# Small-head attentions: two PSUM banks for the scores and three for the turned scores, instead of three and two

## The chip, the cores and the metric

The kernel is one program on one core of a Trainium2 chip. The metric is the device time of one execution in microseconds (us). The core has a matrix engine (PE, TensorE), a vector engine (DVE, VectorE), a scalar engine (ACT, ScalarE), GpSimd (POOL) and DMA queues issued by SyncE (SP). Each engine runs its own instruction list in order and waits on semaphores that others raise. PE writes its results to PSUM, which has eight banks of 512 f32 columns in 128 partitions; DVE and ACT read them there.

## The reference

The program is a stack of four attentions and four feed-forwards on x of shape (4, 512, 128), each added to x. Three of the attentions have 16 heads of 8 channels and take a softmax over all 512 keys, and these are the ones that the change touches:

```python
x = x + _L0_attn_a_ref(_layernorm(x), ...)   # q and k normed per head, no mask
x = x + _L0_ffn_ref(_layernorm(x), ...)      # six layers of windowed attention and feed-forward
x = x + _L0_attn_b_ref(_layernorm(x), ...)   # q, k, v from a latent of 32, causal
x = x + _L0_ffn_ref(_layernorm(x), ...)
x = x + _L1_attn_a_ref(_layernorm(x), ...)   # linear attention
x = x + _L1_ffn_ref(_layernorm(x), ...)
x = x + _L1_attn_b_ref(_layernorm(x), ...)   # causal
x = x + _L1_ffn_ref(_layernorm(x), ...)

scores = einsum('bhsd,bhtd->bhst', q, k) / sqrt(8)
att = softmax(scores); out = einsum('bhst,bhtd->bhsd', att, v)
```

## The kernel before

`build` makes eight stages and `weave` interleaves their programs on each engine: a stage is a generator that yields once per step, and a guest stage starts when its host has taken a given number of steps. `small_attention(core, kind, ...)` is called three times, with kind "norm" (`_L0_attn_a_ref`, the first attention), "latent" (`_L0_attn_b_ref`, the second) and "plain" (`_L1_attn_b_ref`, the third). The other two kinds are causal. Between them runs `local_block` (the six-layer feed-forward), which takes most of the time; `linear_attention` and `swiglu` run ahead of and beside the third attention.

In `small_attention` one step k of the loop is one head of one batch (`ROW_ITEMS` = 4 batches x 16 heads = 64), and the work on a head is spread over steps. The scores are computed twice:

- `scores(k, n_)` (L1228 to L1246): queries on the partitions, keys along the row, in pieces of at most one bank. They serve only to find each query's maximum, which DVE takes from PSUM with `tensor_reduce` (L1463) into `nm`. Each piece raises `s_mm`, each maximum `max_done`.
- once per four heads the 16 maxima of each query are turned by PE (L1288, into `MISC_BANK`), cut into three bf16 parts on DVE (L1471 to L1481) and sent by DMA (L1048) into rows of `qs`.
- `turned_scores(k, n_)` (L1249 to L1265): the same product turned, keys on the partitions, with the negated maximum added by those rows. It runs `LAG` = 7 heads later. ACT takes the exponential from PSUM into `pt` (L1407). Each piece raises `st_mm`, each exponential `exp_done`.
- the value products (L1303) run once per four heads, over three steps: one block, one block, two blocks; then ACT keeps them (L1395) and DVE turns and normalises them (L1486 to L1496).

A head has `NP` pieces: four of 512 columns for "norm" (`q_pieces`, `k_pieces`, one per 128 queries or keys), three in the causal kinds (512; 128 and 384 together; 256), each with a mask product of 128 columns (L1243, L1262) ahead of each part. `Q_BANKS` are the banks through which the score pieces rotate, `K_BANKS` those of the turned pieces; a piece may start when the reader of the bank's last piece is done. With `AV_BANK`, `MISC_BANK` and `ROW_BANK` (the preparation of the next batch) all eight banks are in use.

On PE the order within a step is written out:

```python
for n_ in range(NP):
    if hs is not None:
        scores(hs, n_)
    if n_ == 1 and k % 4 == 0 ...:       # L1288, the maxima turned
    if ht is not None:
        turned_scores(ht, n_)
```

and behind it the value products, the output product (L1312, once per batch) and `prepare(k)` (the layer norm and q, k, v of the next batch, at 6 to 8 of a batch's 16 steps), then the guest stage's step. DVE's order in a step is: the maxima of the head, then in every fourth step the cut of the maxima and the turning of outputs, then its share of the preparation. ACT's order: keeping the products, the exponentials of the head seven earlier, its share of the preparation.

Of the kernel before, what the change touches and what calls it, by code (L numbers as in the profile page):

```python
# [10 lines left out]
ACT = mybir.ActivationFunctionType  # L11
AX = mybir.AxisListType
# [847 lines left out]
def normed_at(g, i):  # L860

    return 3 * g + g // SG + i
# [12 lines left out]
def small_attention(core, kind, local=None, linear=None, source=None):  # L875

    nc, d, x, z, ps = core.nc, core.d, core.x, core.z, core.ps
# [14 lines left out]
    width = 1280 if causal else 2048  # L892
    NP = len(q_pieces)
    if kind == "latent":
        Q_BANKS, K_BANKS, AV_BANK, MISC_BANK, ROW_BANK = (1, 2, 3), (4, 5), 6, 7, 0
    else:
        Q_BANKS, K_BANKS, AV_BANK, MISC_BANK, ROW_BANK = (0, 1, 2), (3, 4), 5, 6, 7
    LAG = 7
    RING = 8
    TURN_VW, MAKE_VW = -25, -24  # L900
# [9 lines left out]
    exp_done, out_kept = ev("sa_exp_done", "sa_out_kept")  # L910
    x_summed, centred, row_done, v_kept, max_done, mcut_done, out_normed, added = ev(
        "n_added", "n_centred", "n_done", "sa_v_kept", "sa_max_done", "sa_mcut_done", "sa_out_normed", "sa_added")
# [13 lines left out]
    def layer_at(k, at):  # L926

        l, s = divmod(k - at, 2)
        return l if kind == "norm" and s == 0 and 0 <= l < DEPTH else None
# [6 lines left out]
    def group_at(k, at):  # L936

        g, s = divmod(k - LAG - at, 4)
        return g if s == 0 and 0 <= g < ROW_GROUPS else None

    def head_at(k, lag):

        return k - lag if 0 <= k - lag < ROW_ITEMS else None
# [21 lines left out]
    nm = prep("nm", [P, 2, 4, TB])  # L965
# [6 lines left out]
    pt = heads_only("pt", [P, RING, width])  # L972
# [174 lines left out]
    def tensor(pe):  # L1147
# [79 lines left out]
        def scores(k, n_):  # L1227

            b, h = divmod(k, SH)
            i_ = NP * k + n_  # L1230
            if kind == "plain" and i_ == 0:
                linear.all_free(pe)
            if n_ == 0 and h == 0:
                pe.wait_ge(ld_low.sem, ld_low.at(16 * loads * (b + 1)))
            if n_ == 0 and h == SH // 2 and b == 0:
                pe.wait_ge(ld_high.sem, ld_high.at(16 * loads))
            if i_ >= 3:
                pe.wait_ge(max_done.sem, max_done.at(i_ - 2))
            bank = ps[:, Q_BANKS[i_ % 3], :]
            for i, col in q_pieces[n_]:  # L1240
                keys = P * (i + 1) if causal else SEQ
                if causal:
                    pe.matmul(bank[:, col + i * P:col + i * P + P], core.ident16[:, :], cmask[:, :], start=True, stop=False, skip_group_check=True)  # L1243
                last = pe.matmul(bank[:, col:col + keys], qs[b % 2][0:STACK, h, i * P:i * P + P], ks[b % 2][0:STACK, h, 0:keys],  # L1244
                                 start=not causal, stop=True, skip_group_check=True)
            last.then_inc(s_mm.sem, 1)  # L1246

        def turned_scores(k, n_):

            b, h = divmod(k, SH)  # L1250
            i_ = NP * k + n_
            if n_ == 0 and h % 4 == 0:
                g = k // 4
                pe.wait_ge(ld_m[g % 2].sem, ld_m[g % 2].at(16 * PARTS * (g // 2 + 1)))
            if i_ >= 2:
                pe.wait_ge(exp_done.sem, exp_done.at(i_ - 1))
            bank = ps[:, K_BANKS[i_ % 2], :]
            for j, col in k_pieces[n_]:
                q0 = P * j if causal else 0
                cols = part[j][1]  # L1260
                if causal:
                    pe.matmul(bank[:, col:col + P], cmask[:, :], core.ident16[:, :], start=True, stop=False, skip_group_check=True)  # L1262
                last = pe.matmul(bank[:, col:col + cols], ks[b % 2][0:M_ROW + PARTS, h, j * P:j * P + P],  # L1263
                                 qs[b % 2][0:M_ROW + PARTS, h, q0:SEQ], start=not causal, stop=True, skip_group_check=True)
            last.then_inc(st_mm.sem, 1)  # L1265

        for k in range(FIRST, LAST):
            if kind == "plain" and k == FIRST + 4:
                local.z_final(pe, BATCH - 1)
                pe.wait_ge(ld_w.sem, ld_w.at(16 * n_ld))  # L1270
                for s in range(3):
                    last = pe.transpose(ROW[:, s * P:s * P + P], tmp[:, s, :], core.ident[:, :])
# [5 lines left out]
# [3 lines that stand above are left out]
                if n_ == 1 and k % 4 == 0 and 0 <= k // 4 - 1 < ROW_GROUPS:  # L1281
                    g = k // 4 - 1
# [8 lines left out]
            for at, blocks in AV_AT.items():  # L1291
                if (g := group_at(k, 4 + at)) is not None:
# [7 lines left out]
                    for j in blocks:  # L1300
                        off, cols = part[j]
                        for hh in range(4):
                            last = pe.matmul(ps[32 * hh:32 * hh + 32, AV_BANK, SEQ - cols:SEQ], va[:, g // SG % 2, j, 4 * (g % SG) + hh, :],  # L1303
                                             pt[:, (4 * g + hh) % RING, off:off + cols], start=j == 0, stop=j == TB - 1, skip_group_check=True)
# [9 lines left out]
            if (l := layer_at(k, TURN_VW)) is not None:  # L1314
# [4 lines left out]
                for c in range(8):  # L1319
                    last = pe.transpose(ps[:, c // 4, c % 4 * P:c % 4 * P + P], wv[l][:, c * P:c * P + P], core.ident[:, :])  # L1320
                last.then_inc(vw_mm.sem, 1)
            if (l := layer_at(k, MAKE_VW)) is not None:
# [5 lines left out]
                for c in range(8):  # L1328
                    for e in range(2):
                        u, j = divmod(2 * c + e, 4)  # L1330
                        rows = slice(64 * e, 64 * e + 64)
                        last = pe.matmul(ps[:, 2 + j, u * P:u * P + P], wvt[l % 2][rows, c, :], wo[l][rows, c, :], start=True, stop=True)
# [3 lines left out]
    def scalar(act):  # L1336
# [46 lines left out]
        for k in range(FIRST, LAST):  # L1383
            if k == FIRST:
                if kind == "latent":
                    local.early_free(act)
                if kind == "norm":
                    act.preload_act_table_set("natural_log_exp_and_others")
            if kind == "latent" and k == LAG:
                local.z_final(act, BATCH - 1)  # L1390
            if (g := group_at(k, 8)) is not None:
                act.wait_ge(av_mm.sem, av_mm.at(g + 1))
                if g >= 2:
                    act.wait_ge(out_normed.sem, out_normed.at(normed_at(g - 2, 1)))
                act.activation(ou[:, g % 2, :], ps[:, AV_BANK, :], ACT.Copy).then_inc(out_kept.sem, 1)  # L1395
            if (h := head_at(k, LAG)) is not None:
                if h == 0 and kind == "norm":
                    for i in range(2):
                        act.wait_ge(vw_stored[i].sem, vw_stored[i].at(16 * DEPTH // 2))
                if h >= RING:  # L1400
                    act.wait_ge(av_mm.sem, av_mm.at((h - RING) // 4 + 1))
                for n_, piece in enumerate(k_pieces):
                    i_ = NP * h + n_
                    col = part[piece[0][0]][0]
                    cols = sum(part[j][1] for j, _ in piece)
                    act.wait_ge(st_mm.sem, st_mm.at(i_ + 1))
                    act.activation(pt[:, h % RING, col:col + cols], ps[:, K_BANKS[i_ % 2], 0:cols], ACT.Exp).then_inc(exp_done.sem, 1)  # L1407
            prepare(k)
            if (l := layer_at(k, TURN_VW)) is not None:
                act.wait_ge(vw_mm.sem, vw_mm.at(2 * l + 1))  # L1410
                act.activation(wvt[l % 2][:, 0:4, :], ps[:, 0, :].rearrange("p (k c) -> p k c", c=P), ACT.Copy).then_inc(vw_kept_act.sem, 1)
            if (l := layer_at(k, MAKE_VW)) is not None:
                act.wait_ge(vw_mm.sem, vw_mm.at(2 * l + 2))
                if l >= 2:
                    act.wait_ge(vw_stored[l % 2].sem, vw_stored[l % 2].at(16 * (l // 2)))
                act.activation(wvo[l % 2][:, 0:2, :], ps[:, 2:4, :], ACT.Copy).then_inc(vw_kept_act.sem, 1)
                act.wait_ge(vw_kept_act.sem, vw_kept_act.at(2 * l + 2))
                act.wait_ge(vw_kept_dve.sem, vw_kept_dve.at(2 * l + 2))
                act.dma_start(core.wvo[l], pt[:, l % 2, :]).then_inc(vw_stored[l % 2].sem, 16)
            yield  # L1420

    def vector(dve):
# [10 lines left out]
        for k in range(FIRST, LAST):  # L1433
# [20 lines left out]
            if (h := head_at(k, 0)) is not None:  # L1454
                g = h // 4
                if h % 4 == 0 and g >= 2:
                    dve.wait_ge(mt_mm.sem, mt_mm.at(g - 1))
                for n_, piece in enumerate(q_pieces):
                    i_ = NP * h + n_
                    dve.wait_ge(s_mm.sem, s_mm.at(i_ + 1))  # L1460
                    for i, col in piece:
                        keys = P * (i + 1) if causal else SEQ
                        last = dve.tensor_reduce(nm[:, g % 2, h % 4, i:i + 1], ps[:, Q_BANKS[i_ % 3], col:col + keys], AX.X, ALU.max, negate=True)  # L1463
                    last.then_inc(max_done.sem, 1)
            if k % 4 == 0 and 0 <= k // 4 - 1 < ROW_GROUPS:
                g = k // 4 - 1
# [105 lines left out]
    def all_free(eng):  # L1572
        eng.wait_ge(added.sem, added.at(BATCH))

    stage = Stage(sync, gpsimd, tensor, scalar, vector)
    stage.early_free, stage.x_final, stage.row_free, stage.all_free, stage.row_bank = early_free, x_final, row_free, all_free, ROW_BANK
    return stage
# [500 lines left out]
```

## Time and profile before

| | |
|---|---|
| time, median of 3 runs | 4424.77 us (4423.37 to 4428.09) |
| time of the profiled execution | 4423.4 us |
| its span | 4421.6 us |
| mean granted TensorE clock | 0.962 |
| PE busy, in the span | 4099.9 us (93%) |
| DVE | 3431.0 us (78%) |
| ACT | 2902.9 us (66%) |
| POOL | 2305.1 us (52%) |
| L1463, maxima (768) | 378.5 us busy, 99.8 us idle before |
| L1407, exponentials (640) | 329.3 us busy, 189.4 us idle before |

The profile is one execution, seen by the hardware profiler. A timeline row gives the start in us from the span's start, the duration in us, the engine, the line of the kernel and the operation with what it writes and reads, how many instructions it merges, and in brackets how long the engine had been idle and what ended that. Several instructions of one line in a row are merged, and their duration is from the first's start to the last's end. A row of a stretch gives, after its bounds and length, the busy time of PE, PE's weight load, DVE, ACT and POOL with the number of instructions (those of one engine alone where only one was asked for), then the granted clock as a share of 2.4 GHz, the DMA share and GB/s. f32 matmuls are recorded as two instructions, and some matmul records are missing.

### The profile page before, as it was taken

Reading aid. Unit: us, or ns where it says so; the run is one execution under the profiler, and the core shown is the slowest. Engines: PE = TensorE matmul, PEld = TensorE weight load, DVE = VectorE, ACT = ScalarE, POOL = GpSimd, SP = SyncE. Lnnn points to the kernel's source line nnn. Section 1 sums busy time; section 2 is a strip of 40 time slices with the busy share of each in tenths; the row PEclk is TensorE's granted clock in tenths of the full one; section 3 lists DMA queues with packets and bytes.
Section 4 is the critical chain, followed back from the end, with each engine's and each line's share of the span. In section 5 each row is a group of like instructions: output and inputs, shape, how many; then the busy total and the mean of one; then the engine's idle time right before and its main releaser. Section 6 shows DMA issues by size and latency. Waiting matters only on the chain. (4 is left out here: it accounts for less than half of the span.)

```text
span 4421.6 us, 128540 instructions
## 1 busy us (share of the span) xinstructions
PE 4099.9 (93%) x53847; PEld 2028.2 (46%) x53847; DVE 3431.0 (78%) x5320; ACT 2902.9 (66%) x7265; POOL 2305.1 (52%) x1444
## 2 busy tenths in 40 slices
PE   5888999999999999998989999999999999988897
PEld 3222555555555554553434555555554555543442
DVE  3774888888888888885868888888888888865783
ACT  2654777777777777774546777777777777755453
POOL 3101766666666666664107666666666666631100
PEclk7987999999999999997989999999999999999898
DMA  5112000000000000001220000000000000001110
GB/s 167 48 30 63 2 2 26 3 21 7 21 7 2 21 7 2 2 2 45 67 66 7 2 21 7 21 7 2 26 2 21 7 2 2 2 10 32 44 45 10
DMA packets 68917, 97.79 MB, mean 22 GB/s; under 512 B 34472, under 2 KB 58756, under 8 KB 62340
## 3 DMA queue, kind: packets, MB, share of 16 engines
q1 hardware_dynamic: 67476, 83.28, 6.4%
q8 instruction: 426, 6.98, 0.7%
q10 hardware_dynamic: 864, 6.29, 0.4%
q14 instruction: 151, 1.24, 0.1%
HBM read 72.18 MB, written 16.78 MB: 20 GB/s over the span
## 5 line engine op out<-in xcount | busy, mean ns | idle before, releaser
L402 POOL TENSOR_TENSOR ra<-ra,rb 128x1024 f32<-128x1024 f32 x384 | 927.3, 2415 | 330.4 <-DVE rb L741 330.4
L416 POOL TENSOR_TENSOR qkr<-ra,inv 128x1024 f32<-128x1024 f32 x384 | 730.9, 1904 | 607.8 <-ACT inv L680 604.1
L448 PE MATMUL ps<-wvo,xs 128*32 128x512 f32 x6144 | 821.2, 606 | 72.2 <-ACT vs L602 72.2
L493 PE MATMUL ps<-wq,xs 128*128 128x512 f32 x1536 | 748.3, 610 | 6.2 <-DVE rb L741 3.5
L653 ACT ACTIVATE pr<-ps,neg 128x64 f32<-128x64 f32 x3072 | 668.1, 337 | 7.1 <-DVE neg L718 7.1
L602 ACT ACTIVATE vs<-ps 128x512 f32<-128x512 f32 x768 | 450.8, 587 | 227.2 <-PE ps L448 225.9
L515 PEld LDWEIGHTS ps<-kt,qt 64*32 64x32 f32 x24576 | 360.5, 107 | 293.8 <-issue 290.1
L718 DVE TENSOR_REDUCE neg<-ps 128x8 f32<-128x512 f32 x384 | 263.7, 687 | 279.8 <-PE ps L515 272.9
L493 PEld LDWEIGHTS ps<-wq,xs 128*128 128x128 f32 x1536 | 274.6, 191 | 431.6 <-issue 333.8
L738 DVE TENSOR_TENSOR ra<-ps,rope 128x1024 f32<-128x1024 f32 x384 | 451.7, 1176 | 24.3 <-ACT sq L627 17.3
L741 DVE TENSOR_TENSOR rb<-ps,rope 128x1024 f32<-128x1024 f32 x384 | 465.7, 1213 | 0.0
L764 DVE TENSOR_REDUCE ssq<-sq 128x16 f32<-128x1024 f32 x384 | 464.2, 1209 | 0.0
L541 PEld LDWEIGHTS ps<-vs,pt 128*32 128x32 f32 x11904 | 346.2, 110 | 239.9 <-issue 215.8
L1463 DVE TENSOR_REDUCE nm<-ps 128x1 f32<-128x512 f32 (+3 forms) x768 | 378.5, 549 | 99.8 <-PE ps L1244 97.7
L1407 ACT ACTIVATE pt<-ps 128x512 f32<-128x512 f32 (+1 forms) x640 | 329.3, 552 | 189.4 <-PE ps L1263 182.9
L435 POOL TENSOR_TENSOR pn<-pr,rden 128x512 f32<-128x512 f32 x384 | 400.4, 1043 | 47.3 <-DVE rden L724 41.7
L515 PE MATMUL ps<-kt,qt 64*32 64x64 f32 x24576 | 422.4, 218 | 0.3 <-DVE kt L772 0.3
L669 ACT ACTIVATE inv<-ssq 128x16 f32<-128x16 f32 x384 | 82.8, 216 | 507.5 <-DVE ssq L779 507.5
L541 PE MATMUL ps<-vs,pt 128*32 128x128 f32 x11904 | 407.2, 273 | 4.2 <-DVE pt L789 4.2
L627 ACT ACTIVATE sq<-ps 128x1024 f32<-128x1024 f32 x384 | 390.6, 1017 | 29.1 <-PE ps L493 28.0
L659 ACT ACTIVATE qt<-ps 128x512 f32<-128x512 f32 x384 | 244.5, 637 | 66.4 <-PE ps L560 62.5
L1244 PE MATMUL ps<-ks,qs 72*128 72x512 bf16 (+3 forms) x768 | 255.1, 354 | 26.0 <-DVE nm L1463 25.9
(253 smaller groups left out, 6246.0 us busy)
## 6 DMA issues: line engine op xcount, KB each, us to landing
wq<-in_L_ffn_Wqkv SPq DMA_DIRECT2D x12, 1024.0 KB, 5.2
wvo<-wvo_scratch SPq DMA_DIRECT2D x12, 1024.0 KB, 4.9
wvo_scratch<-pt ACTq DMA_DIRECT2D x6, 1024.0 KB, 4.0
w<-in_L_ffn_W SPq DMA_DIRECT2D x12, 341.0 KB
qs<-norm_pieces SPq DMA_DIRECT2D x9, 384.0 KB
ks<-norm_pieces SPq DMA_DIRECT2D x9, 384.0 KB
qs<-latent_pieces SPq DMA_DIRECT2D x9, 384.0 KB
ks<-latent_pieces SPq DMA_DIRECT2D x9, 384.0 KB
```

Source lines behind the costliest of these rows:

```text
L402: pool.tensor_tensor(ra[:, m % 2, :, :], ra[:, m % 2, :, :], rb[:, :, :], ALU.add).then_inc(sum_done.sem, 1)
L416: pool.tensor_tensor(qkr[:, m % 2, :, :].rearrange("p s (h c) -> p (s h) c", c=HD), ra[:, m % 2, :, :].rearrange("p s (h c) -> p (s h) c", ...
L435: pool.tensor_tensor(pn[:, m % 2, :, :], pr[:, m % 2, :, :], rden[:, m % 2, :, None].to_broadcast([P, 8, KEYS]), ALU.mult).then_inc(pn_don ...
L448: last = pe.matmul(VP[32 * j:32 * j + 32, :], xs[:, turn % 2, v * WIN:v * WIN + WIN], wvo[l % 2][:, j, :], start=True, stop=True)
L493: last = pe.matmul(PJ[:, qk, :], xs[:, turn % 2, t * P:t * P + P], wq[l % 2][:, at:at + 512], start=True, stop=True)
L515: last = pe.matmul(SB[32 * j:32 * j + 32, at:at + KEYS], qt[rows, m % 2, (2 * i + p) * TB + w, :], kt[rows, 4 * up + 2 * i + p, t * P + w ...
L541: last = pe.matmul(PO[32 * w:32 * w + 32, t * P:t * P + P], pt[:, m % 2, i * TB + w, half, :], vs[:, v, 2 * up + i, :], start=up == 0 and ...
L602: act.activation(vs[:, v, :, :].rearrange("p u c -> p (u c)"), VP, ACT.Copy).then_inc(v_kept.sem, 1)
L653: last = act.activation(pr[:, m % 2, n, :], SB[:, n * KEYS:n * KEYS + KEYS], ACT.Exp, bias=neg[:, m % 2, n:n + 1])
L738: dve.tensor_tensor(ra[:, m % 2, :, :].rearrange("p s (h c) -> p s h c", c=HD), both, table, ALU.mult)
L741: dve.tensor_tensor(rb[:, :, :].rearrange("p s (h e c) -> p s h e c", h=8, e=2), halves, tableh, ALU.mult).then_inc(rope_done.sem, 1)
L764: dve.tensor_reduce(ssq[:, m % 2, :], sq[:, :, :].rearrange("p s (h c) -> p (s h) c", c=HD), AX.X, ALU.add).then_inc(ss_done.sem, 1)
```

## The change

In both cases of the bank layout, one bank moves from `Q_BANKS` to `K_BANKS`. The indices and the two waits follow: a score piece waits for the maximum of the piece two earlier instead of three, a turned piece for the exponential of the piece three earlier instead of two. Nothing else differs.

```diff
     if kind == "latent":
-        Q_BANKS, K_BANKS, AV_BANK, MISC_BANK, ROW_BANK = (1, 2, 3), (4, 5), 6, 7, 0
+        Q_BANKS, K_BANKS, AV_BANK, MISC_BANK, ROW_BANK = (1, 2), (3, 4, 5), 6, 7, 0
     else:
-        Q_BANKS, K_BANKS, AV_BANK, MISC_BANK, ROW_BANK = (0, 1, 2), (3, 4), 5, 6, 7
+        Q_BANKS, K_BANKS, AV_BANK, MISC_BANK, ROW_BANK = (0, 1), (2, 3, 4), 5, 6, 7
...
-            if i_ >= 3:
-                pe.wait_ge(max_done.sem, max_done.at(i_ - 2))
-            bank = ps[:, Q_BANKS[i_ % 3], :]
+            if i_ >= 2:
+                pe.wait_ge(max_done.sem, max_done.at(i_ - 1))
+            bank = ps[:, Q_BANKS[i_ % 2], :]
...
-            if i_ >= 2:
-                pe.wait_ge(exp_done.sem, exp_done.at(i_ - 1))
-            bank = ps[:, K_BANKS[i_ % 2], :]
+            if i_ >= 3:
+                pe.wait_ge(exp_done.sem, exp_done.at(i_ - 2))
+            bank = ps[:, K_BANKS[i_ % 3], :]
```

In the same way L1407 reads `K_BANKS[i_ % 3]` and L1463 reads `Q_BANKS[i_ % 2]`.

## Rows read from the trace of the kernel before

**Rows 1.** Busy time by stretch: the three loops from first to last L1471.

```profile
102.80:362.70 259.90, 225.58 (x957) 60.12 (x956) 193.24 (x376) 146.96 (x260) 22.58 (x17) 0.86 0.16 44
2091.10:2264.70 173.60, 162.39 (x1419) 81.76 (x1418) 145.15 (x378) 99.54 (x199) 14.85 (x11) 0.96 0.22 63
4132.30:4334.10 201.80, 182.16 (x1460) 91.36 (x1458) 158.46 (x390) 110.73 (x213) 14.74 (x10) 0.95 0.17 46
```

**Rows 2.** Timeline of PE, first attention, one group at full clock.

```profile
300.24 0.39 PE L1244 MATMUL ps<-ks,qs 72*128 72x512 bf16 x1 [1.32 <-DVE nm L1463]
300.47 0.38 PE L1263 MATMUL ps<-qs,ks 75*128 75x512 bf16 x1
...
301.77 0.39 PE L1244 MATMUL ps<-ks,qs 72*128 72x512 bf16 x1
...
303.94 1.93 PE L1303 MATMUL ps<-pt,va 128*32 128x512 f32 x16
```

**Rows 3.** Timeline of DVE in the same group.

```profile
296.70 0.27 DVE L1471 COPY mf<-ps 16x128 f32<-16x128 f32 x1
...
299.50 2.48 DVE L1463 TENSOR_REDUCE nm<-ps 128x1 f32<-128x512 f32 x4
302.20 2.48 DVE L1463 TENSOR_REDUCE nm<-ps 128x1 f32<-128x512 f32 x4 [0.23 <-PE ps L1244]
306.23 4.88 DVE L1463 TENSOR_REDUCE nm<-ps 128x1 f32<-128x512 f32 x8 [1.54 <-PE ps L1244]
311.02 0.27 DVE L1471 COPY mf<-ps 16x128 f32<-16x128 f32 x1
```

**Rows 4.** Timeline of DVE, then of PE, second attention, one group.

```profile
2193.36 3.27 DVE L1463 TENSOR_REDUCE nm<-ps 128x1 f32<-128x512 f32 x8
2197.15 1.70 DVE L1463 TENSOR_REDUCE nm<-ps 128x1 f32<-128x512 f32 x4 [0.53 <-PE ps L1244]
...
2201.02 0.27 DVE L1471 COPY mf<-ps 16x128 f32<-16x128 f32 x1
...
2194.10 0.23 PE L1243 MATMUL ps<-cmask,ident 128*128 128x128 bf16 x1 [0.22 <-DVE nm L1463]
...
2195.88 0.86 PE L1303 MATMUL ps<-pt,va 128*32 128x256 f32 x16
2196.67 0.23 PE L1243 MATMUL ps<-cmask,ident 128*128 128x128 bf16 x1
```

**Rows 5.** Timeline of PE, first attention, two preparing heads.

```profile
179.48 0.39 PE L1263 MATMUL ps<-qs,ks 75*128 75x512 bf16 x1 [1.32 <-ACT pt L1407]
...
199.49 0.39 PE L1263 MATMUL ps<-qs,ks 75*128 75x512 bf16 x1 [0.58 <-ACT pt L1407]
```

**Rows 6.** Timeline of DVE, first attention, heads without turned scores.

```profile
93.14 9.79 DVE L1463 TENSOR_REDUCE nm<-ps 128x1 f32<-128x512 f32 x16
```

**Rows 7.** Timeline of PE in the three tails, one after the other.

```profile
363.64 0.61 PE L1263 MATMUL ps<-qs,ks 75*128 75x512 bf16 x1 [0.41 <-ACT pt L1407]
...
395.96 1.10 PE L1263 MATMUL ps<-qs,ks 75*128 75x512 bf16 x2 [0.32 <-ACT pt L1407]
...
2278.66 0.29 PE L1262 MATMUL ps<-ident,cmask 128*128 128x128 bf16 x1 [3.94 <-DMA qs<-mcut]
...
2292.86 0.23 PE L1262 MATMUL ps<-ident,cmask 128*128 128x128 bf16 x1 [0.41 <-ACT pt L1407]
...
4338.19 0.23 PE L1262 MATMUL ps<-ident,cmask 128*128 128x128 bf16 x1 [0.56 <-ACT pt L1407]
...
4343.98 0.29 PE L1262 MATMUL ps<-ident,cmask 128*128 128x128 bf16 x1 [3.95 <-ACT pt L1407]
...
4362.75 0.23 PE L1262 MATMUL ps<-ident,cmask 128*128 128x128 bf16 x1 [0.41 <-ACT pt L1407]
```

**Rows 8.** Busy time of two neighbouring groups, first attention.

```profile
299.50:313.80 14.30, 12.68 (x66) 3.24 (x66) 12.29 (x26) 9.43 (x18) 0.00 (x0) 1.00 0.01 3
313.80:331.00 17.20, 15.72 (x66) 3.75 (x66) 12.53 (x26) 9.60 (x18) 0.10 (x1) 0.80 0.00 1
```

More of the change, by code:

```diff
@@ L1406, in scalar @@
                     act.wait_ge(st_mm.sem, st_mm.at(i_ + 1))
-                    act.activation(pt[:, h % RING, col:col + cols], ps[:, K_BANKS[i_ % 2], 0:cols], ACT.Exp).then_inc(exp_done.sem, 1)
+                    act.activation(pt[:, h % RING, col:col + cols], ps[:, K_BANKS[i_ % 3], 0:cols], ACT.Exp).then_inc(exp_done.sem, 1)
             prepare(k)
@@ L1462, in vector @@
                         keys = P * (i + 1) if causal else SEQ
-                        last = dve.tensor_reduce(nm[:, g % 2, h % 4, i:i + 1], ps[:, Q_BANKS[i_ % 3], col:col + keys], AX.X, ALU.max, negate=True)
+                        last = dve.tensor_reduce(nm[:, g % 2, h % 4, i:i + 1], ps[:, Q_BANKS[i_ % 2], col:col + keys], AX.X, ALU.max, negate=True)
                     last.then_inc(max_done.sem, 1)
```

## The prediction

> **What bounds the kernel now.** The change touches only the loop over 64 heads in the three small-head attentions, so I began with the busy time per stretch, one stretch for each of the three [rows 1]. No engine is full: in the first, PE is busy for 225.6 of 259.9 us and DVE for 193.2; in the second 162.4 and 145.2 of 173.6; in the third 182.2 and 158.5 of 201.8. ACT is well below. Two engines near the top and neither full means that they wait for each other in turn, so shares say nothing and one repeating group has to be read instruction by instruction. A group is four heads. Names from here on: S0 to S3 are the score pieces of a head, T0 to T3 the turned pieces of the head seven earlier, R the maximum on DVE, E the exponential on ACT; the heads of a group are A, B, C, D, and D is the one after which DVE leaves the loop. PE's order is S0 T0 S1 T1 S2 T2 S3 T3, then the value products.
>
> The first attention's group at full clock [rows 2, 3]: DVE starts its side work (the cut of the maxima, the turning of outputs) at 296.70 and returns at 299.50, 2.80 later; the next side work starts at 311.02, so a group takes 14.32 us. While DVE is away PE fills the three score banks and stops: S3 of head A starts at 300.24 after 1.32 us idle, 0.74 after the start of the first R. So the bound is DVE's sum (its maxima and its side work) plus the gaps in which PE comes too late, 0.23 ahead of 302.20 and 1.54 ahead of 306.23. In both, PE was in the value products. What shortens those gaps is how far PE had run ahead in scores, and that is what the number of score banks sets.
>
> **The change part by part.** No instruction is added or taken away. Two waits move: S now waits for the R two pieces back (was three), T for the E three pieces back (was two). Behind a waiting S on PE stand T, the value products and everything woven in; behind a waiting T the same. The step is worked by replaying one group with the durations of the rows. From them [rows 2, 3]: one R after another 0.60 (eight in 4.88, four in 2.48); start of R to the S that it frees 0.74; start of S to its R 0.43 (301.77 to 302.20); S to T 0.23 or less; T3 to the next head's S0 1.30 with one block of value products (300.47 to 301.77), about 0.3 of it ahead of the products; two blocks take 1.86 from their start (303.94) to S0, since R of head C starts at 306.23, 0.43 behind S0.
>
> *First attention, one group, times from 299.50.* Before: S3 of A 0.74, S0 of B 2.27, R of B 2.70, R of C 6.73, side work 11.52. After: only S0 and S1 of A are in banks. S2 waits for R0: 0.74; T2 0.97; S3 waits for R1: 1.34; T3 1.57; S0 of B 1.57 + 1.30 = 2.87, and R 3.30 (was 2.70). In B, S2 waits for R0: 4.04, S3 for R1: 4.64, T3 4.87; products from 5.18, S0 of C 7.04, R 7.47 (was 6.73). In C and D each S is freed at 0.74 and ready 0.43 later, 1.17 against two R of 1.20, so DVE barely runs on, apart from one slip where the maxima's transposition (0.33) stands between S1 and S2 of D: R2 at 11.30 where 11.07 was due. Side work starts at 12.50, **0.98 later** in a group of 14.32. The turned side gives back little here: T2 no longer waits for E0, but S3 behind it waits for R1 anyhow.
>
> *Causal attentions.* The same replay [rows 4]: times from 2193.36: head A's S2 starts at 0.74 instead of ahead of the group; with T2 and one block  (0.77, as the two short ones, 2195.88 to 2196.67) S0 of B is at 1.94 and R, 0.48 behind it, at 2.42 (was 1.61: eight R run unbroken in 3.27). S2 of B waits for R0 (3.16), products and S0 of C follow at 3.61 and 4.40 (was 3.31), R 4.88 (2197.15: 3.79). C and D took 3.87 before, from 2197.15 to 2201.02, with waits for T2 in them; the replay gives 3.77, as T2 no longer waits but S2 and the next S0 do. The side work comes at 8.65 against 7.66, **0.99 later** in 10.46.
>
> *How many groups.* Each stretch has 15. In three batches of four, one attention prepares the next batch between heads, about two groups each time. There ACT is late and PE stands before T2, three times per batch: the first and the last of the three are 1.32 and 0.58 us, the middle one 0.41 [rows 5]. With a third turned bank T2 goes at once; S3 then waits for R1, so I get back 0.6, 0.5 and 0.3, say 1.4 of two times 0.98. So a stretch loses 9 x 0.98 + 3 x 0.56 = 10.5, and three lose **31.5 us**.
>
> *Heads before the turned scores begin.* With no T between, DVE has run 16 R without a gap (9.79 us) [rows 6], and here S's 1.17 against 1.20 holds only at full clock. At half clock the 0.22 between two pieces doubles, so S to R is about 0.65 and a piece 0.1 longer: +1.5 us. In the causal ones S0 of the next head waits for the double R1 and reaches DVE 0.27 late, seven heads, +1.9 each. Together **+5.3**, between nothing and twice that.
>
> *Tails.* In the last seven heads there are only T, E and products; PE waits for E at T2. These waits are 6.6 us in the first attention (seven rows between 363.64 and 395.96), 2.5 in the second behind 2278.66 (three rows up to 2292.86; what was gained ahead of 2278.66 is lost, since there T0 waits for a DMA), 5.9 in the third (five rows from 4338.19 to 4362.75) [rows 7]. A third bank removes nearly all; I take 12 of 15, since some of it meets another wait. One long ACT block (SiLU's three passes) lies inside the third loop; its twin in the tail holds T2 for 3.95 (4343.98), and while scores still run I take 2 of that. **-14**.
>
> Sum: 31.5 + 5.3 - 14 = **+23**.
>
> *Clock.* In the first attention a group at full clock is 14.3 us, its neighbour with a stretch at 1.2 GHz 17.2 [rows 8]. The stretches' means are 0.86, 0.96 and 0.95 [rows 1]. In the causal group PE's longest gap was 0.22 us (ahead of 2194.10); in the replay PE stands from 10.6 to 12.2, 1.6 us, more than the 1.32 that the first attention had. If both causal stretches fell to 0.86, about 75 us more would be at half rate, and by the two rows (0.20 of 17.2 below full is 6.9 us at half rate, costing 2.9) each such us costs 0.42: +32; the first attention falling by 0.06 more adds 14. Bounds 0 to +46, and a gain is excluded since PE's idle time grows in every replay. I take a quarter, **+12**: the gap is once per group and the causal stages hold full clock now with gaps of that order only at the preparing steps.
> The Trainium skill, "TensorE: Matmul & The Clock Gate", section "A second HAM failure mode: psum-queue depth-cycling", says that a PE which pauses briefly between groups as it cycles through PSUM banks has its clock swing between half and full rate. It speaks against this change, and by it the sum would be +69 rather than +35. The first attention's rows agree with it; the causal group's, with the same cycling at full clock, do not.
>
> +23 + 12 = **+35**. The profiled execution has a span of 4421.6 and a time of 4423.4, the median is 4424.8; 4424.8 + 35 = 4460.
>
> **The rivals.** (a) *The clock follows the idle time.* As above, all of it: +23 + 46 = +69, 4494. For it: the first attention, where 0.86 over 260 us at 6.9 us each makes some ten of fifteen groups with a half-rate stretch. Against: the causal groups' other gaps are tiny. (b) *ACT was the late one.* If DVE's lead can be rebuilt in C and D, because PE no longer stands before T2, the group's loss vanishes and what is left is 5.3 - 14 - 9 x 1.4 = -21, 4404. It decides where E is later than R when PE reaches S2; for it speak the T2 waits in C and D [rows 5, 7], against it that DVE, not ACT, has no slack in a group (12.3 of 14.3 us busy, ACT 9.4) [rows 8]. (c) *They cancel.* If a group loses half of what the replay says, 45 x 0.98 = 44 becomes 22 and the sum without the clock is +1, 4426. (d) *The wait isn't reached*: PE never gets three ahead. Excluded by the 300.24 row: S3 of A waited, so S0 to S2 were all in.
>
> **How the numbers follow.** Forecast 4460 (+25 to +50): 0.60. (a) 0.20. (c) 0.11. (b) 0.08. (d) 0.01. A measurement of this kernel tells about 0.2% (9 us) from no change. Slower by more: forecast and (a), and a little of (c), 0.82; within: 0.10; faster: 0.08. The range leaves out (b), part of (c) and the far end of (a): 4426 to 4500.
>
> **What would show it.** In the profile of the changed kernel: in a full-clock group of the first attention S2, not S3, of head A is the piece that starts 0.74 after DVE returns; side work to side work 15.3 (first) and 11.4 (causal); DVE's idle ahead of L1463 up by about 30 us over the three, ACT's waits for L1263 in the body about as before; PE's waits for L1407 ahead of L1263 and L1262 mostly gone, those for L1463 ahead of L1244 and L1243 up. The last score piece of each attention later by 10 to 16 us, the stretch from there to the next stage shorter by 2 to 6. Wrong if the distance between side works is unchanged (b), or if the granted clock of the causal stretches falls under 0.90 (a).

## The result: 1.2% slower

The changed kernel takes 4479.7 us in the median of four runs (4471.3 to 4483.6) against 4426.4: a ratio of 1.0119, 95% interval 1.0101 to 1.0136, 53 us. The forecast was 4460, the range 4426 to 4500. The result is 20 us above the forecast and 14 below rival (a)'s 4494. The profiled execution has a span of 4478.1 and a time of 4479.8, 56.5 us of span more than before. These are rows of its page: the busy times, the granted clock in 40 slices (in tenths) and the maxima's line.

```profile
span 4478.1 us, 128540 instructions
...
PE 4121.5 (92%) x53847; PEld 2034.5 (45%) x53847; DVE 3438.8 (77%) x5320; ACT 2903.1 (65%) x7265; POOL 2305.4 (51%) x1444
...
PEclk8888999999999999997889999999999999999988
...
L1463 DVE TENSOR_REDUCE nm<-ps 128x1 f32<-128x512 f32 (+3 forms) x768 | 383.7, 551 | 156.0 <-PE ps L1244 150.3
```

PE has 22 us more busy time with the same instructions (some of its matmuls ran at the lower clock), and DVE's idle time ahead of L1463 went from 99.8 to 156.0 us. The three loops from first to last L1471, to be laid beside [rows 1]:

```profile
103.40:382.50 279.10, 237.29 (x958) 59.49 (x958) 197.04 (x376) 147.11 (x260) 22.59 (x17) 0.82 0.15 41
2099.50:2301.10 201.60, 172.99 (x1419) 87.95 (x1419) 146.61 (x377) 101.05 (x199) 14.85 (x11) 0.90 0.19 55
4165.00:4392.80 227.80, 193.85 (x1462) 97.77 (x1461) 159.54 (x389) 111.78 (x213) 14.72 (x10) 0.89 0.15 41
```

They are 19.2, 28.0 and 26.0 us longer, and their mean granted clock fell from 0.86, 0.96 and 0.95 to 0.82, 0.90 and 0.89. In the listing by lines, PE's idle time behind DVE ahead of the score pieces (L1244, L1243) went from 38.8 to 104.7 us, and that behind ACT ahead of the turned pieces (L1263, L1262) from 36.4 to 11.0. Where the 56.5 us of the span lie (each distance is between two rows of the timelines: the first and the last L1471 of a loop, and the next stage's first L493; for the third tail the end of the span):

| us | before | after | difference |
|---|---|---|---|
| up to the first loop's first L1471 | 102.8 | 103.4 | +0.6 |
| first loop | 259.8 | 279.0 | +19.2 |
| first tail | 51.3 | 37.5 | -13.8 |
| up to the second loop's first L1471 | 1677.1 | 1679.6 | +2.4 |
| second loop | 173.6 | 201.6 | +28.0 |
| second tail | 41.9 | 34.3 | -7.6 |
| up to the third loop's first L1471 | 1825.7 | 1829.6 | +3.9 |
| third loop | 201.8 | 227.8 | +26.0 |
| third tail | 87.5 | 85.3 | -2.2 |

One causal group at full clock, beside [rows 4]; DVE first, then PE:

```profile
2264.85 0.27 DVE L1471 COPY mf<-ps 16x128 f32<-16x128 f32 x1
...
2267.65 1.68 DVE L1463 TENSOR_REDUCE nm<-ps 128x1 f32<-128x512 f32 x4
2270.10 1.70 DVE L1463 TENSOR_REDUCE nm<-ps 128x1 f32<-128x512 f32 x4 [0.78 <-PE ps L1244]
2272.57 1.70 DVE L1463 TENSOR_REDUCE nm<-ps 128x1 f32<-128x512 f32 x4 [0.76 <-PE ps L1244]
2274.55 1.91 DVE L1463 TENSOR_REDUCE nm<-ps 128x1 f32<-128x512 f32 x4 [0.28 <-PE ps L1244]
2276.37 0.27 DVE L1471 COPY mf<-ps 16x128 f32<-16x128 f32 x1
...
2268.39 0.23 PE L1243 MATMUL ps<-cmask,ident 128*128 128x128 bf16 x1 [1.42 <-DVE nm L1463]
...
2269.61 0.23 PE L1243 MATMUL ps<-cmask,ident 128*128 128x128 bf16 x1
...
2272.08 0.23 PE L1243 MATMUL ps<-cmask,ident 128*128 128x128 bf16 x1
```

DVE returns at 2267.65. S2 of head A starts 0.74 later, after PE stood for 1.42 us; S0 of B follows at 1.96, of C at 4.43; their maxima at 2.45 and 4.92. The replay had 0.74, 1.94, 4.40, 2.42 and 4.88. The side work comes at 8.72 (replay 8.65), and group to group is 11.52. The usual full-clock group of this attention was 10.31 before (2223.7 to 2234.0 for one).

### The profile page after: what moved, and what is told of

Same layout as the page of the kernel before. It is cut to its first block and busy times, and to the rows that moved or that the text cites. A ratio compares the mean times of both kernels' runs of the same rounds, so it can differ in the third digit from the quotient of the medians.

```text
span 4478.1 us, 128540 instructions
## 1 busy us (share of the span) xinstructions
PE 4121.5 (92%) x53847; PEld 2034.5 (45%) x53847; DVE 3438.8 (77%) x5320; ACT 2903.1 (65%) x7265; POOL 2305.4 (51%) x1444
## 5 line engine op out<-in xcount | busy, mean ns | idle before, releaser
L493 PE MATMUL ps<-wq,xs 128*128 128x512 f32 x1536 | 748.2, 610 | 6.3 <-DVE rb L741 3.7
L1463 DVE TENSOR_REDUCE nm<-ps 128x1 f32<-128x512 f32 (+3 forms) x768 | 383.7, 551 | 156.0 <-PE ps L1244 150.3
L1407 ACT ACTIVATE pt<-ps 128x512 f32<-128x512 f32 (+1 forms) x640 | 330.5, 554 | 249.7 <-PE ps L1263 243.6
L493 PEld LDWEIGHTS ps<-wq,xs 128*128 128x128 f32 x1536 | 274.6, 191 | 432.0 <-issue 334.8
L1244 PE MATMUL ps<-ks,qs 72*128 72x512 bf16 (+3 forms) x768 | 269.3, 370 | 42.9 <-DVE nm L1463 39.6
```

The source lines that it names most:

```text
L493: last = pe.matmul(PJ[:, qk, :], xs[:, turn % 2, t * P:t * P + P], wq[l % 2][:, at:at + 512], start=True, stop=True)
```

## The experiments

All times below are medians on a chip that ran the kernel before beside them (4425.6, 4426.6 and 4429.2 us in the three sessions). "Half-rate time" is the part of a stretch at the lower granted clock: twice its length times one less the mean clock (taken with three digits, where the rows show two). The rows of loops are of one profiled execution each; the medians are of 4 to 14.

### Half of the change: two score banks, two turned banks

```diff
-        Q_BANKS, K_BANKS, ... = (0, 1), (2, 3, 4), 5, 6, 7
+        Q_BANKS, K_BANKS, ... = (0, 1), (3, 4), 5, 6, 7      # bank 2 idle; (1, 2), (4, 5) in the latent kind
```

and the turned pieces wait as before, two back.

> Two banks for the scores, two for the turned scores, one bank idle: only the first half of the change. Theory (the lost score bank does the harm in the bodies, the third turned bank pays back only in the tails): the bodies are about as long as in the changed kernel (279, 202 and 228 us from first to last L1471), the tails are as long as before (51, 42 and 87 us against 38, 34 and 85), so about 24 us slower than the changed kernel, near 4504 us. Rival (the third turned bank also carries the bodies, since T2 no longer blocks PE): the bodies get longer by 0.4 us or more a group, another 20 us, near 4525 us. Rival (the harm is in the third turned bank or its new wait): faster than the changed kernel, near 4430 us.

4505.5 us, ratio 1.0181 (1.0166 to 1.0197). The loops:

```profile
105.00:384.00 279.00, 240.01 (x958) 62.69 (x957) 195.54 (x375) 148.99 (x260) 22.56 (x17) 0.83 0.15 42
2111.30:2319.20 207.90, 179.13 (x1419) 89.48 (x1419) 147.03 (x378) 101.61 (x199) 14.85 (x11) 0.88 0.20 54
4186.50:4410.80 224.30, 187.82 (x1462) 93.70 (x1461) 159.08 (x390) 112.55 (x213) 14.73 (x10) 0.92 0.15 42
```

279.0, 207.9 and 224.3 us, with the changed kernel's 279.1, 201.6 and 227.8: the lost score bank alone lengthens the loops, and the third turned bank gives at most a few us back there. It removed what it should: over the three loops PE's waits for ACT ahead of turned pieces are 1.9 us in the changed kernel, 10.6 here and 18.5 in the kernel before. But in the loops PE waited for the maxima instead. The tails are 49.3, 33.9 and 89.2 us. The second of them is as short as in the changed kernel though it has two turned banks. It isn't short in the same way: here PE waits 6.3 us for ACT and not at all for the transfer of the last maxima, at a clock of 0.99; in the changed kernel it waits 0.4 us for ACT and 3.4 for the transfer, at 0.84.

### Where PE's order hurts: the value block ahead of S2

The block of value products that head A had behind its last turned piece is issued inside the loop over pieces, while PE would stand for DVE:

```diff
             for n_ in range(NP):
+                if n_ == 2:                      # NP - 1 in the kernel before
+                    value_blocks(2, AV_AT[2])
                 if hs is not None:
                     scores(hs, n_)
```

First in the changed kernel.

> The changed kernel, with the single value block that head A had behind its last turned piece put ahead of its S2, into the time in which PE stands there anyway. Theory (PE comes too late because everything behind S2, the value block too, is pushed behind DVE's return): S0 of B comes 0.99 earlier in the first attention and 0.5 in the causal ones, 0.9 and 0.5 us a group, 16 and 32 groups, 30 us, and up to 12 more from the clock since PE's longest gap shrinks: 4437 to 4450 us. Rival (PE's order doesn't matter, DVE is short of banks all along the group): under 10 us gained, 4470 or more.

4418.0 us, ratio to before 0.9986 (0.9977 to 0.9996); 62 us less than the changed kernel.

```profile
104.40:353.30 248.90, 219.62 (x958) 57.23 (x958) 195.71 (x375) 146.87 (x260) 22.60 (x17) 0.89 0.17 46
2067.80:2259.50 191.70, 172.13 (x1419) 87.95 (x1419) 146.57 (x377) 101.36 (x199) 14.85 (x11) 0.90 0.20 57
4125.70:4333.20 207.50, 181.71 (x1462) 93.82 (x1461) 159.35 (x389) 111.83 (x213) 14.73 (x10) 0.94 0.16 45
```

Full-clock groups fell from 15.3 us (read below, in the kernel with seven products) to 14.4 in the first attention and from 11.5 to 11.0 in the causal ones, 0.9 and 0.5 as expected, which settles that the loss of a group was PE's work queued behind S2. The loops are 60 us shorter, of which the groups make some 31. The rest goes with the clock, for which I had allowed 12: half-rate time in the three loops fell from 192 to 118 us (54, 40 and 24). In the second loop it stayed at 40, though its gap was filled too.

The same edit in the kernel before, ahead of S3 in the first attention and of S2 in the causal ones:

> The kernel before, with the same value block of head A put ahead of its last score piece. In the first attention PE stands 1.32 us ahead of S3 of A; filled with the block of 0.99, S0 of B comes at 1.28 instead of 2.27, and R of C at about 5.97 instead of 6.73: 0.76 us a group, 12 us in 16 groups. Clock theory (PE's gap of over a microsecond is what drops it): the gap falls to about 0.35, most of the ten half-rate stretches of 2.9 us go, another 15 to 29 us: 4385 to 4400 us. Rival (the clock doesn't follow this gap): only the 12 us, 4414 us. The causal attentions stay within 2 us, as there was no gap ahead of their S2.

4388.2 us, ratio 0.9922 (0.9905 to 0.9938). One group of the first attention, DVE, then PE, and the first two loops:

```profile
282.16 4.87 DVE L1468 TENSOR_REDUCE nm<-ps 128x1 f32<-128x512 f32 x8
288.11 4.88 DVE L1468 TENSOR_REDUCE nm<-ps 128x1 f32<-128x512 f32 x8 [1.08 <-PE ps L1244]
292.90 0.27 DVE L1476 COPY mf<-ps 16x128 f32<-16x128 f32 x1
...
282.90 0.39 PE L1244 MATMUL ps<-ks,qs 72*128 72x512 bf16 x1 [0.32 <-DVE nm L1468]
```

```profile
100.90:333.00 232.10, 208.82 (x957) 57.64 (x956) 192.78 (x375) 147.22 (x260) 22.60 (x17) 0.93 0.17 48
2057.40:2232.20 174.80, 164.12 (x1419) 82.94 (x1418) 145.51 (x377) 101.19 (x199) 14.86 (x11) 0.95 0.22 63
```

The gap ahead of R of B is gone (eight maxima from 282.16), that ahead of R of C is 1.08, R of C comes 5.95 after DVE's return (expected 5.97, before 6.73), and PE's gap is 0.32 instead of 1.32. A full-clock group is 13.54 us instead of 14.32, and the loop has a clock of 0.93 instead of 0.86. It is 28 us shorter, of which 12 are the groups; the rest came with the clock (half-rate time 34 us instead of 73). The second loop is 1.2 us longer, the third 3.0 shorter, within and a little beyond the 2 us expected.

### The clock by itself: products that nobody reads

In the changed kernel, extra bf16 products of 512 columns go to `MISC_BANK` ahead of S2 of head A. They add work and free nothing.

```diff
             for n_ in range(NP):
+                if n_ == 2 and k % 4 == 1 and k >= 5 and hs is not None:
+                    pe.wait_ge(mcut_done.sem, mcut_done.at(6 * (k // 4 - 1) + 1))
+                    for _ in range(4):           # 7 in the second version
+                        pe.matmul(ps[:, MISC_BANK, :], ks[...], qs[...], start=True, stop=True)
```

> The changed kernel with four extra bf16 products of 512 columns (0.88 us at full clock, result never read, into the bank of the turned maxima) ahead of S2 of head A, where PE stands 2.2 us (first attention) and 1.4 us (causal) for DVE's return. They add work and free nothing. Clock theory (half the loss of the change is half-rate time that follows this gap; by 0.42 us per us at half rate): half-rate time in the three bodies falls from 101, 40 and 51 us to about half, and the time by about 30 us, 4450. Rival (the clock has nothing to do with the gap, the longer groups are all queueing): half-rate time unchanged, 4480 or slower.

4455.9 us, ratio 1.0071 (1.0056 to 1.0086), 24 us less than the changed kernel. Half-rate time in the loops is 70, 27 and 24 us instead of 101, 40 and 51.

> The same with seven extra products (1.54 us at full clock). Clock theory: the first attention's gap of 2.2 us shrinks to about 0.6, its half-rate time falls further than with four; in the causal ones 1.54 us no longer fit into 1.4, S2 of A comes 0.1 us late in full-clock groups, 2 to 4 us lost: between 4440 and 4460. Rival (queueing only): slower than with four by what doesn't fit, 4485 or more.

4444.7 us, ratio 1.0047 (1.0032 to 1.0062): 35 us less. A group of the first attention, DVE, then PE; and the loops:

```profile
299.47 2.48 DVE L1467 TENSOR_REDUCE nm<-ps 128x1 f32<-128x512 f32 x4
302.77 2.48 DVE L1467 TENSOR_REDUCE nm<-ps 128x1 f32<-128x512 f32 x4 [0.82 <-PE ps L1244]
306.93 5.12 DVE L1467 TENSOR_REDUCE nm<-ps 128x1 f32<-128x512 f32 x8 [1.68 <-PE ps L1244]
311.97 0.27 DVE L1475 COPY mf<-ps 16x128 f32<-16x128 f32 x1
...
327.28 0.27 DVE L1475 COPY mf<-ps 16x128 f32<-16x128 f32 x1
...
313.19 1.67 PE L1282 MATMUL ps<-qs,ks 72*128 72x512 bf16 x7
315.51 0.39 PE L1244 MATMUL ps<-ks,qs 72*128 72x512 bf16 x1 [0.64 <-DVE nm L1467]
```

```profile
103.00:360.30 257.30, 236.02 (x1063) 65.60 (x1063) 195.31 (x376) 146.72 (x260) 22.60 (x17) 0.92 0.16 44
2078.10:2269.20 191.10, 183.45 (x1524) 93.12 (x1524) 145.78 (x378) 100.89 (x199) 14.85 (x11) 0.97 0.20 57
4133.30:4353.30 220.00, 204.25 (x1566) 102.95 (x1565) 159.29 (x389) 111.94 (x213) 14.73 (x10) 0.95 0.15 42
```

Seven products take 1.67 us of PE's gap, and 0.64 is left. With the clock held, the first attention's group can be read clean: from DVE's return at 299.47, R of B is at 3.30, R of C at 7.46, side work at 12.50, and side work to side work is 15.31. The replay of [rows 2, 3] had 3.30, 7.47, 12.50 and 15.30.

And the kernel before with four such products, ahead of S3 of head A and in the first attention alone (`n_ == 3`):

> The kernel before with four such products ahead of S3 of head A, in the first attention alone, where PE stands 1.3 us. Nothing else moves. Clock theory: half-rate time in that body falls from 73 to under 40 us and the time by about 14 us, 4412, which would put more than a third of what moving the value block brought (38 us) on the clock. Rival (that gain was queueing alone): 4426, no change.

4408.4 us, ratio 0.9961 (0.9946 to 0.9976), 18 us less than before.

```profile
100.80:348.10 247.30, 224.19 (x1017) 61.98 (x1016) 193.78 (x376) 145.89 (x260) 22.56 (x17) 0.92 0.16 46
2074.70:2248.20 173.50, 162.33 (x1419) 81.76 (x1418) 145.10 (x377) 99.50 (x199) 14.86 (x11) 0.96 0.21 62
4119.30:4321.10 201.80, 182.21 (x1459) 91.35 (x1457) 158.44 (x390) 110.64 (x213) 14.74 (x10) 0.95 0.17 46
```

Half-rate time in the first loop fell from 73 to 41 us, and full-clock groups stayed at 14.3. The profiled execution's first loop is 12.6 us shorter.

These two give the split. The kernel before with four products and the changed one with seven have nearly the same half-rate time, 41, 13 and 21 us against 39, 13 and 24. Their loops differ by 10.0, 17.6 and 18.2 us: that is the queueing, 46 us. (Up to 3 of it may be the products themselves: with four instead of seven the third loop is 217.2 us, at the same half-rate time.) Taking the products away again costs the changed kernel 35 us and the kernel before 18, so the clock makes the difference between them 17 us larger; it is 36 with the clock held and 53 without. The intervals of the four ratios leave that 17 uncertain by about 12. By the spans of the profiled executions it is 25: 56.5 without the products, 31.3 with them.

### The third turned bank at a held clock

The seven products in the kernel with two banks for each kind.

> Two banks for each kind, one idle, with the seven extra products ahead of S2 of head A that hold the clock. Against the changed kernel with the same seven products (4445 us, half-rate time 75 us in the bodies) only the third turned bank differs, at about the same clock. Theory (the third turned bank does nothing in a full-clock group and a little at the preparing heads, and works in the tails of the first and third attention): bodies within 3 us each of 257, 191 and 220, tails of the first and third 12 and 4 us longer, 4460 to 4466. Rival (it also carries the bodies): bodies 5 us or more longer each, 4475 or more.

4476.2 us, ratio 1.0104 (1.0089 to 1.0119), 31 us more than with the third turned bank, above what I expected and past the rival's bound in time. The loops fit neither: I expected each within 3 us, the rival 5 or more longer. The profiled execution was the fastest of its four (4466.6), and in it the loops are 256.6, 195.6 and 223.9 against 257.3, 191.1 and 220.0 us, the tails 10.5, 2.6 and 3.0 longer. So the third bank is worth about 8 us in the loops and 16 in the tails. In the loops it works at the preparing heads: two such groups of the second attention are 14.8 and 18.7 us instead of 13.9 and 16.5, and a full-clock group without preparation gains 0.07 in the causal ones and nothing in the first. The first loop's preparing groups gain 2.6 us too; that doesn't show in its length, since the kernel with three turned banks has 6 us more at half rate there. What the other 6 us of the medians are, I can't say from one profile.

### The tails

In the kernel before, with the loops as they were, the turned pieces use all five banks once there are no scores left:

```diff
+    TAIL = NP * (ROW_ITEMS - LAG)
+    FREED = Q_BANKS + tuple(K_BANKS[(TAIL + n) % 2] for n in range(2))
+    def turned_bank(i_):
+        return FREED[(i_ - TAIL) % 5] if i_ >= TAIL else K_BANKS[i_ % 2]
```

with the first of them behind all maxima, and from the fourth on each behind the exponential of the piece five back.

> The kernel before (three and two banks), but in the last seven steps, where there are no scores any more, the turned pieces rotate over all five banks. Theory (the changed kernel's shorter tails come from PE no longer standing before T2): the tails shorten by what they did in the changed kernel or a little more, 13.7, 7.6 and 2.2 us, the bodies stay: 4400 to 4406 us. Rival (those tails were shorter only since the bodies ended later and DMAs and layer norms had caught up): the tails stay at 51, 42 and 87 us, 4424 us.

4405.8 us, ratio 0.9961 (0.9948 to 0.9974); tails 32.5, 36.5 and 85.4 us. So it is true that tails can be shortened through banks. But in the first tail, where most of the changed kernel's gain lies, the reason that I had given isn't what its rows show. PE in that tail, the first and the last of six waits behind ACT; then the first tail as a stretch, before and after:

```profile
387.25 0.39 PE L1263 MATMUL ps<-qs,ks 75*128 75x512 bf16 x1 [1.38 <-ACT pt L1407]
...
405.20 0.39 PE L1263 MATMUL ps<-qs,ks 75*128 75x512 bf16 x1 [0.32 <-ACT pt L1407]
```

```profile
362.70:414.00 51.30, 38.74 (x137) 8.48 (x137) 13.24 (x29) 21.73 (x40) 2.78 (x6) 0.71 0.08 28
```

```profile
382.50:420.00 37.50, 25.82 (x138) 6.82 (x136) 13.23 (x29) 20.96 (x40) 2.78 (x6) 1.00 0.10 37
```

The six waits are 6.1 us together, the seven of before were 6.6 [rows 7]. They moved from T2 to T3 and cost as much. What changed is the clock: 0.71 before, 1.00 after, 30 us of half-rate time against none. PE's busy time is 12.9 us less, about the 13.8 of the tail. It goes with the banks in all profiles: the six kernels with two turned banks in this tail take 47.0 to 51.3 us, with 20 to 30 at half rate, the four with three take 36.3 to 38.4, with 0 to 4, and the three with five take 31.8 to 34.9, with 0 to 7. How the third bank keeps the clock up here isn't shown.

In the other two tails the waits for ACT did go, from 5.3 to 0.4 us and from 5.9 to 2.7, as predicted. The second tail is 7.6 us shorter, the third only 2.2, with 3 us more at half rate.

The second tail is also a matter of the transfer that brings the last maxima, [rows 7] at 2278.66. SP's issues of the kernel before around it:

```profile
2258.17 0.51 SPq L334 DMA_DIRECT2D wq<-in_L_ffn_Wqkv  x1
...
2270.76 0.43 SPq L337 DMA_DIRECT2D wvo<-wvo_scratch  x1
2271.23 1.89 SPq L1048 DMA_DIRECT2D qs<-mcut  x3
```

SP issues the next stage's loads from 2258.17 on, thirteen by its rows, and gets to the maxima only at 2271.23, behind the last load of 1 MB, though DVE had them ready at 2266.3. In the kernel with five banks PE got there earlier and stood the longer:

```profile
2272.37 0.29 PE L1272 MATMUL ps<-ident,cmask 128*128 128x128 bf16 x1 [6.48 <-DMA qs<-mcut]
```

The changed kernel still waits for it, less long:

```profile
2311.39 0.29 PE L1262 MATMUL ps<-ident,cmask 128*128 128x128 bf16 x1 [3.37 <-DMA qs<-mcut]
```

That is 10.3 us behind its last L1471, where it was 14.0 before: SP had begun the loads 9.6 us ahead of that L1471 instead of 6.5. So 3.7 of the second tail's 7.6 us lie ahead of this row, and 3.9 behind it.

So I sent those loads one step later:

```diff
-            if k == -PRE:
+            if k == -PRE + 1:
                 attention.early_free(sp)
                 load_wq(0)
```

> The kernel before, with the twelve loads that the next stage issues on SP (weights, tables) one step later, so that the last group's maxima are sent ahead of them. Theory (the 3.94 us that PE stands ahead of the last group's turned scores in the second attention, and the short second tail of the changed kernel, come from the maxima's transfer standing behind those loads on SP): that wait is gone, the second tail is 37 to 39 us instead of 41.9, the first tail within 1 us of before, 4421 to 4424 in all. Rival (the maxima's transfer is slow by itself): no change in the tail; and if the weights now come too late, the next stage starts later, 4430 or more.

4420.1 us, ratio 0.9978 (0.9968 to 0.9987).

```profile
2280.61 0.23 PE L1262 MATMUL ps<-ident,cmask 128*128 128x128 bf16 x1 [1.31 <-ACT pt L1407]
...
2282.95 0.23 PE L1262 MATMUL ps<-ident,cmask 128*128 128x128 bf16 x1 [0.49 <-ACT pt L1407]
```

The transfer wait is gone (T2 of the step before and then T2 of the last group's first head are what waits), and the second tail is 35.8 us instead of 41.9: 6 us shorter, where 3 to 5 were expected. The median is 9 us lower. In the profiled execution, the slowest of ten, the first loop is 268.1 us instead of 259.8, though nothing in it changed, and the first tail 2.1 us shorter, against 1 expected:

```profile
101.30:369.40 268.10, 235.64 (x957) 62.31 (x956) 193.86 (x376) 147.66 (x260) 22.59 (x17) 0.82 0.12 35
```

Its clock is 0.82 where [rows 1] have 0.86. The kernel with five banks had 271.3 us in that loop, at 0.81.

### Together

> The two helpful edits together on the kernel before: the value block of head A ahead of its last score piece, and the turned pieces over all five banks in the tails. If body and tail are independent, the gains of 38 and 20 us add up: 4366 to 4372 us. If the tails gain less when the bodies end earlier (they meet DMAs or the next stage's layer norms), 4375 to 4388.

4371.6 us, ratio 0.9877 (0.9860 to 0.9893). 55 us less than before, with 37 and 20 for the parts: they add up within their intervals.

> All three edits that stay with three score banks: the value block of head A early, the turned pieces over five banks in the tails, the next stage's loads behind the last maxima. In the kernel with the first two the transfer wait in the second tail is hidden by nothing else, so the third edit should bring 3 to 6 us there: 4365 to 4369 against 4371.6. Rival (the tail is then set by the next stage's layer norm chain): 4371.

4353.8 us, ratio 0.9835 (0.9820 to 0.9850). The third edit brought 18 us, three times what I expected. The second tail is 26.4 us instead of 36.5: the wait of 6.5 us for the transfer is gone, and so are 13 of 14 us at half rate. What the other 8 us are isn't shown. The profiled execution with the first two edits was the slowest of its four, and the stretches ahead of the second and third loops, which the third edit shouldn't touch, differ by 3.8 and 3.6 us between the two profiles. This kernel keeps three score banks and two turned ones in the loops and is faster than both kernels of the change.

## Why the prediction was right, point by point

**The sign and the step that carried it held.** S2 instead of S3 of head A waits for DVE's return, and all of PE's list behind it moves. The replay of one group was exact in the first attention: 0.98 predicted, 0.99 measured (15.31 against 14.32). For the causal group 0.99 was predicted and 1.2 measured (11.52 against 10.31, the usual group; the one that I replayed was 10.46, because of a T2 wait that most groups lack).

**But the time is inside the range because misses partly cancel.** The loss was 53 us where 35 were forecast: queueing and clock were both larger than my terms and the tails gave back more. The prediction had named a sign by which its clock term would be wrong, a granted clock of the causal stretches under 0.90. They had 0.899 and 0.888. That the time is inside the range is in part luck; the mechanism, the sign and the first attention's group are not.

**How many groups lose: right in the first attention, too low in the causal ones.** 10.5 us per loop were predicted; with the clock held it was 10.0, 17.6 and 18.2. The step that failed is the term for preparing groups, 0.56 for two of them, 1.7 a loop. PE's rows show six groups with preparation work in each loop (the first to third and the fifth to seventh), so their number was right, though it is twice three and not three times two. Between the kernels with filled gaps, and with the half-rate stretches that each group happens to have:

| us lost | predicted, each | first | second | third |
|---|---|---|---|---|
| six preparing groups | 1.7 | 1.7 | 5.3 | 8.8 |
| nine others | 8.8 | 8.4 | 12.3 | 9.4 |

Without the third turned bank the six lose 4.3, 9.0 and 9.1 us, where I had 5.9, and the bank gives 2.6, 3.7 and 0.3 back, where I had 4.2. The sum came out right in the first attention with both parts too high. The three T2 waits were rows of the first attention [rows 5], and I carried them to the causal kinds without reading a row there. In the causal kinds a head has three pieces, T2 is its last, and the score piece behind it is the next head's; that this is why they lose more is argued, not shown.

**Heads without turned scores**: +5.3 predicted, 0.6 + 2.4 + 3.9 = 6.9 in the stretches that hold them, by the two profiles of the table. The last of the three says little: that stretch takes 1825.7 to 1829.7 us in the seven kernels with three score banks, and 1829.6 in the changed one. Against those seven as a whole some 4 us are left. This was not tried alone.

**The tails: -14 predicted, -24 measured, and only in part for the reason given.** PE's waits for ACT in the three tails went from 6.6, 5.3 and 5.9 us to 6.1, 0.4 and 2.7. That is 8.6 us, where I had taken 12. In the first tail, with 13.8 of the 24 us, they moved from T2 to T3, and it got shorter with its half-rate time, 30 us before and none after, a term that the prediction had only for the loops. In the second, half the gain lies ahead of the last maxima's transfer: SP's order is the same, and what differs is how far DVE's last maxima lie behind the loads.

**The clock: the other term that was mis-sized.** I took 12 us out of 0 to 46. Half-rate time in the loops rose from 106 to 192 us, 86 us, and by the 0.3 us that each cost between the changed kernel with and without seven products (35 us for 117), that is 26; by the experiments with filled gaps 17 of the 53 us, give or take 12. Against the forecast's +35, the causal loops' queueing is +15, the clock +5 to +14, the tails -10, the early heads about nothing. Rival (a) named this mechanism; it came to about half of what (a) allowed. My reason for a quarter was that the causal stages hold full clock with such gaps at their preparing steps. They don't have one in every group, and when they got one (1.42 us) the clock of both fell from about 0.95 to 0.90. The rule that I had quoted from the Trainium skill, "TensorE: Matmul & The Clock Gate", section "A second HAM failure mode: psum-queue depth-cycling", that brief pauses between groups as PE cycles through PSUM banks make its clock swing, is borne out here: with the pauses partly filled by useless products the first loop's clock was 0.92 instead of 0.86 before and 0.82 after, and both kernels were faster.

**The rivals that fell.** (b), ACT late, would have needed the third turned bank to carry the loops; at a held clock it brings 8 us of some 660. (c), half the loss per group, fell with 0.99 measured.

**What stays open**: the 6 us between medians and profiled execution of the two-and-two kernel with products; why the preparing groups of the causal loops lose more; why the third turned bank keeps the first tail at full clock; and why the value block, which took half-rate time from the changed kernel's first and third loops, took none from the second.

## What to carry to other kernels

These are rules from one kernel. When two readers of PSUM share the matrix engine through one in-order list, give the banks to the reader that leaves the loop for side work, not to the one with more idle time: the number of its banks is how far PE gets ahead while it is away, and everything behind the first refused piece is pushed past its return. Before banks are moved, look at what stands behind that piece: work that needs nothing from it belongs ahead of it, in the pause. And once one kind of piece has ended, let the other use all banks.

## What the runs showed of the hardware

A pause of PE of 1.3 us (before) or 2.2 us (after) once per group of 14 to 20 us cost more than itself. In the first attention of the kernel before, the mean granted clock of a loop with such pauses was 0.86, and 0.9 us of products that nobody reads raised it to 0.92 and took 18 us off the kernel. A pause in each group doesn't always do it: four groups of the changed kernel's second loop had 1.4 us of it and full clock. Whether a given group falls to 1.2 GHz differs between executions and between kernels that are the same up to there: that loop took 259.8, 268.1 and 271.3 us in three profiles of identical instructions, with 73, 96 and 103 us at half rate. Such a loop's time in one profile can't be compared to better than 10 us without its clock beside it.
